# Scores of a 64-key cross-attention on 64-row tiles of TensorE instead of the full 128-row array

## The reference

```python
q = hidden_state @ Wq + bq          # 32 query heads of 32
k = encoder_hidden_state @ Wk + bk  # 8 key heads of 32
scores = jnp.einsum('bkgld,bksd->bkgls', q, k) * scale
scores = scores + encoder_attention_mask[:, :, None, :, :]
attn = jax.nn.softmax(scores, axis=-1)
```

## Time and profile before

| | us |
|---|---|
| median of 3 runs | 1916.51 |
| lowest, highest | 1906.94, 1917.58 |
| the profiled execution's own time | 1914.38 |
| its span in the trace | 1912.6 |
| mean granted TensorE clock of the span | 0.978 |

### The profile page before, as it was taken

One profiled execution on the slowest core, in us unless ns is written; L12 is line 12 of the kernel. 1 busy time (PEld: TensorE's weight loads), 2 busy tenths in 40 slices (PEclk: granted clock), 3 DMA queues, 4 the chain that ended last, 5 costly groups with the idle time before them and its releaser, 6 DMA issues.

```text
span 1912.6 us, 22864 instructions
## 1 busy us (share of the span) xinstructions
PE 1791.6 (94%) x8832; PEld 1486.5 (78%) x8832; DVE 1073.9 (56%) x1070; ACT 578.7 (30%) x664; POOL 1029.4 (54%) x576
## 2 busy tenths in 40 slices
PE   5999999999988899999999967999999999999998
PEld 5788888888876778788778856887788778877887
DVE  6888888888867344444444454345534554455432
ACT  3444444444434432333233312113211321122110
POOL 2677777777759745565654664225522552254221
PEclk9999999999999999999999988999999999999999
DMA  8423332333263466556757745414341434142110
GB/s 206 111 75 82 81 83 70 80 85 77 52 194 113 132 220 205 193 189 207 240 188 233 228 136 154 154 67 126 95 154 66 128 93 154 66 135 86 66 56 33
DMA packets 250476, 244.48 MB, mean 128 GB/s; under 512 B 61952, under 2 KB 205440, under 8 KB 250368
## 3 DMA queue, kind: packets, MB, share of 16 engines
q1 hardware_dynamic: 249216, 241.97, 41.6%
q10 hardware_dynamic: 1152, 1.05, 0.2%
HBM read 157.99 MB, written 84.93 MB: 127 GB/s over the span
## 4 chain that ended last, share of the span: by engine, by line
PE 54%; DVE 20%; issue 9%; ACT 6%; DMA 4%; POOL 3%; SPq 3%; ACTq 0%; DVEq 0%
PE ps L53 17%; PE ps L54 16%; PE ps L55 16%; DVE small L998 3%; DVE pr L1021 3%; ACT pr L765 3%; DVE pT0r L1032 2%; DVE pT1r L1032 2%; DVE xT0r L928 2%; PE ps L672 2%; ACT ot L759 2%; DVE xT1r L928 1%; PE ps L616 1%; DVE x2r L1104 1%; PE ps L624 1%
## 5 line engine op out<-in xcount | busy, mean ns | idle before, releaser
L1299 POOL TENSOR_TENSOR prob<-prob,small 128x1024 f32<-128x1024 f32 x32 | 61.1, 1908 | 397.9 <-DVE small L1115 397.9
L1235 POOL TENSOR_TENSOR pr<-pr,small 128x1024 f32<-128x1024 f32 x64 | 122.0, 1906 | 100.8 <-DVE small L1027 100.8
L1111 DVE SCALAR_TENSOR_TENSOR prob<-ps,bias 128x1024 f32<-128x1024 f32 x32 | 39.1, 1222 | 227.6 <-PE ps L55 227.6
L866 ACT CAST x2Th<-x2r 128x1024 fp32r<-128x1024 f32 x32 | 33.6, 1050 | 424.7 <-DVE x2r L1104 424.7
L1251 POOL TENSOR_TENSOR xb<-xb,bo 128x1024 f32<-128x1024 f32 x32 | 79.4, 2483 | 150.0 <-DMA xb<-in_x_dram 149.7
L1230 POOL TENSOR_TENSOR pr<-pr,small 128x1024 f32<-128x1024 f32 x64 | 124.0, 1937 | 34.4 <-DVE small L1002 34.2
L998 DVE TENSOR_REDUCE small<-pr 128x16 f32<-128x1024 f32 x64 | 78.1, 1220 | 90.7 <-ACT pr L765 90.7
L1074 DVE TENSOR_TENSOR y<-ps,xb 128x512 f32<-128x512 f32 x64 | 43.9, 687 | 126.1 <-PE ps L55 122.9
L53 PE MATMUL ps<-wo0h,oc0l 128*128 128x512 f32 x256 | 104.2, 407 | 1.7 <-DVE wo0l L952 1.7
L1043 DVE TENSOR_TENSOR y<-y,gam 128x1024 f32<-128x1024 f32 x32 | 51.6, 1612 | 92.2 <-ACT y L798 92.2
L53 PE MATMUL ps<-wo0h,oc1l 128*128 128x512 f32 x256 | 103.1, 403 | 0.0
(11 more groups left out here) (318 smaller groups left out, 5526.1 us busy)
## 6 DMA issues: line engine op xcount, KB each, us to landing
o_scratch<-ot SPq DMA_DIRECT2D x256, 64.0 KB, 1.8
ocr<-o_scratch SPq DMA_DIRECT2D x16, 1024.0 KB, 7.0
xb<-in_x_dram SPq DMA_DIRECT2D x32, 512.0 KB, 6.5
x_scratch<-y SPq DMA_DIRECT2D x32, 512.0 KB, 4.7
a_scratch<-ost SPq DMA_DIRECT2D x64, 256.0 KB, 3.3
b_scratch<-ost SPq DMA_DIRECT2D x64, 256.0 KB, 4.6
xd<-x_scratch SPq DMA_DIRECT2D x128, 128.0 KB, 2.9
raw<-b_scratch SPq DMA_DIRECT2D x64, 256.0 KB, 7.5
```

Source lines behind the costliest of these rows:

```text
L1235: nc.gpsimd.tensor_tensor(heads(v), heads(v), mx.unsqueeze(2).to_broadcast([P, TPB * GRP, KEYS]), ALU.subtract)\
L1299: nc.gpsimd.tensor_tensor(prob[:], prob[:], mx1.unsqueeze(2).to_broadcast([P, H1, KEYS]), ALU.subtract)\
```

## The change

The 128-row matmul of a token tile is split in two by rows: rows 0 to 63 hold heads 0 and 1, rows 64 to 127 hold heads 2 and 3. Each half is a matmul of 64 rows and 128 moving columns (two heads of 64 keys), issued alternately, three terms each, in the same order of terms. A unit has 24 such matmuls. The half r writes bank r of `S`, so the order in a unit's two banks becomes (head j, tile m, key), which is the order of `pr`; DVE's addition of the mask reads and writes in that order, with the mask of the block repeated over heads.

```diff
--- before.py
+++ after.py
@@ -542,8 +542,13 @@
                     pe.wait_ge(k_ld[v % 2], 16 * GRP * (v // 2 + 1))
                     after(pe, s_read, v - 1)
                     for m in range(TPB):
-                        last = three(nc, S[v % 2][:, 256 * m:256 * (m + 1)], [qs[v % 2][x][:, m] for x in (0, 1)],
-                                     [kb[v % 2][:, :, x] for x in (0, 1)], True, True)
+                        for i, (x, z) in enumerate(((1, 0), (0, 1), (0, 0))):
+                            for r in range(2):
+                                rows = slice(2 * HD0 * r, 2 * HD0 * (r + 1))
+                                last = nc.tensor.matmul(S[v % 2][:, HALF * r:HALF * (r + 1)]
+                                                        .rearrange("p (j m s) -> p m j s", j=2, m=TPB)[:, m],
+                                                        qs[v % 2][x][rows, m], kb[v % 2][rows, 2 * r:2 * r + 2, z],
+                                                        start=i == 0, stop=i == 2)
                     last.then_inc(scores, 1)
                 if u < UNITS:
                     query(range(4, KT))
@@ -1018,10 +1023,10 @@
                     if v % KT == 0:
                         dve.wait_ge(mask_ld, 16 * (t + 1))
                     dve.wait_ge(scores, v + 1)
-                    nc.vector.tensor_tensor(p[:].rearrange("p j m s -> p m j s"),
-                                            S[v % 2].rearrange("p (m j s) -> p m j s", m=TPB, j=GRP),
-                                            mask[t % 2][:].unsqueeze(2).to_broadcast([P, TPB, GRP, KEYS]), ALU.add)\
-                        .then_inc(s_read, 1)
+                    nc.vector.tensor_tensor(p[:].rearrange("p j m s -> p j (m s)"),
+                                            S[v % 2].rearrange("p (j c) -> p j c", j=GRP),
+                                            mask[t % 2][:].rearrange("p m s -> p (m s)").unsqueeze(1)
+                                            .to_broadcast([P, GRP, TPB * KEYS]), ALU.add).then_inc(s_read, 1)
                     dve.wait_ge(s_read, v + 1)
                     after(dve, centered, v)
                     nc.vector.tensor_reduce(mx, p[:].rearrange("p j m s -> p (j m) s"), AX_X, ALU.max).then_inc(maxed, 1)

```

## The result

| | us |
|---|---|
| changed kernel, median of 20 runs (lowest to highest) | 1914.72 (1908.74 to 1921.52) |
| kernel before, median of 20 runs | 1910.37 (1905.81 to 1917.58) |
| ratio, 95% interval | 1.0025 (1.0013 to 1.0036) |
| span of the profiled execution, mean granted clock | 1911.4, 0.974 |

The change makes the kernel slower by 2.5 to 6.9 us, 4.35 between the medians, against 1.6 forecast. The time lies in the range, and the sign is the forecast's.

The account below looks back on a forecast made before the run. DVE, ACT and POOL, at 17.13 us a pair of slots, were taken to bound the kernel, hiding PE's growth to 17.04. Six PE-bound slots add 1.6: 1914.4 becomes 1916.0, with 2.1 for the median 1918; range 1909 to 1928.

Parts of the forecast that it names:

- What bounds the kernel: First layer's slots: DVE, ACT and POOL set 17.13 us a pair of slots; PE needs 16.52 and has 0.61 spare.
- the ring: Cycle of DVE, ACT and POOL work in a pair of slots, mask addition to token transpose, repeating every 17.13 us.
- The block: A unit's scores on PE: 12 pairs of 64-row matmuls at 0.108 us, 1.30 in place of 1.44, a gain of 0.14.
- In and out: Entering and leaving the 64-row tiles on PE loses 0.20 us each way, 0.40 in each of 64 units.
- The cover: PE's wait for the queries' low part hides its longer slot over 23 pairs; without it 0.26 a slot, 12 us.
- The mask addition: DVE's addition in the new order, 64 times: 0 to +2.9 us, taken as 0.
- The size: Whole kernel: 1.6 us slower, from 0.26 in each of some six slots that PE bounds.
- the pair at 0.118: First rival, score block: PE just becomes the bound, pair of slots 17.28, +5.8 us, 1922; chance 0.20.
- the full gain at 0.066: Second rival, score block: matmul pairs take 0.066 us, only six slots gain, -1.5 us, 1915; chance 0.08.
- the pair that costs two steps: Third rival, score block: a matmul pair takes 0.216 us, pair of slots 19.62, about +70 us, 1988; chance 0.11.
- the clock: Fourth rival: PE's idler array lets its clock fall in each third pair of slots, +16 us, 1934; chance 0.04.

Follow-up runs that it names:

- one term: Kernel before with only the high by high product of the scores, 4 matmuls of 256 columns a unit in place of 12: 1905.65 us.
- the swap: Kernel before with ACT's exponential ahead of the output copy in each slot, nothing changed on PE: 1889.63 us.
- two blocks: Changed kernel with a unit's scores in two blocks of 12 matmuls, six full-row projection matmuls between them: 1926.36 us.
- full-row cut: Kernel before with each full-row score matmul of 256 columns cut into two of 128 columns, 24 a unit, no tiles: 1971.68 us.
- the loops exchanged: Changed kernel with, per token tile, the three terms of rows 0 to 63 written before the three of rows 64 to 127: 1914.52 us, one execution.
- the old order of the mask addition: Changed kernel with DVE's mask addition walking in the order token tile, head, key, tiles unchanged: 1918.54 us, one execution.
- one term with the swap: Kernel before with only the high by high score product and ACT's exponential ahead of the output copy: 1882.03 us.
- the swap with tiles: Changed kernel with ACT's exponential ahead of the output copy: 1907.68 us.

## Why the prediction was right

- *What bounds the kernel*: right, and shown from three sides. Less work on PE leaves the period at 17.12 (one term), a shorter ring without a change on PE takes it to 16.52 (the swap), and a longer PE raises it only once its slot passes the ring (two blocks, 17.68).
- *The block*: 12 pairs at 0.108 were expected and 0.112 measured. The full-row cut shows the same 0.112 without any tiling. That the load sets it fits the 0.11 of an exposed load, and is argued, not shown by a run.
- *In and out*: 0.20 us each way was read from the tables, and an unwaited block shows the same way in: the full matmul that starts at 524.22 ends 0.227 later, and the first pair, loaded from 524.54 on, begins 0.11 after that, a gap of 0.20. The way out was taken from the tables at 0.20 and is 0.14 here. The experiment with two blocks puts the real addition at 0.31 a block. That the sum came out so close, 8.53 against 8.52, is in part luck: the underestimate of the pairs (12 x 0.004 = 0.05) and the overestimate of the way out (0.06) have opposite signs.
- *The cover*: right. The 23 pairs of slots lost 17.17 - 17.13 = 0.04 us each, while PE still had 0.11 us to spare in each. Without the cover the tiles cost 18 us.
- *The mask addition*: nothing, as taken; 1.173 against 1.176 us over the same stretch.
- *The size*: too small. 1.6 us forecast, 4.35 measured (2.5 to 6.9). In the profiled executions the last scores start 606.86 - 602.61 = 4.25 us later. Of it, 1.1 us are the ring's 0.04 (the token transposes, a term that the sum did not have), 0.95 us lie between 513.19 and 546.34, where PE bounds, as forecast, and 1.8 us are there by slot 8, at 121.02 against 119.25. Half of this last part, 0.96 us, is there before the first scores (47.93 against 46.97), and 0.82 of it already at the first query projection, where nothing was changed (below). The rest, 0.5 us, is at the end of the layer.
- *Rivals*: the pair at 0.118, the full gain at 0.066, the pair that costs two steps, and the clock are all out: 0.112, 0.112, 0.112, and a mean clock of 0.974 against 0.978. The first rival was nonetheless near. Its condition, a pair of slots over the ring's, fails by 17.13 - 17.06 = 0.07 us.

The first matmul of the query projection before:

```profile
38.68 0.40 PE L53 MATMUL ps<-xT0h,wq0l 128*128 128x512 f32 x1
```

and after:

```profile
39.50 0.47 PE L53 MATMUL ps<-xT0h,wq0l 128*128 128x512 f32 x1
```

Most of this 0.82 us is not an accident of one execution. The profiled executions of the six kernels with 24 score matmuls a unit (the changed one, full rows, and the other four with tiles) start this matmul at 39.17 to 39.50 us, those of the four with 12 or 4 at 38.68 to 38.80. The prediction had no term for this, and its cause stays open.

## What to carry to other kernels

A busy share of 94% on an engine does not say that a shorter operation on it pays: look for the period in the starts of a repeated instruction and compare it with the stretch in which nothing is waited for. The steady slots here held 0.61 us of wait in 17.13, enough to hide a step that became 0.27 us a slot worse, and DVE's long wait for the exponential pointed to the swap of two ACT operations that was worth 1%. At 128 columns a pair of 64-row tiles brought a step of 0.120 us down to 0.112 and no further, about what an exposed weight load takes (0.11), and the ways in and out came on top, some 0.3 us a block.

## What the runs showed of the hardware

An fp32r matmul of 128 columns with its own weights takes 0.112 us at the full clock, about as long as an exposed load of 128 columns delays its matmul (498.86 to 498.97, 0.11). The Trainium skill, "TensorE: Matmul & The Clock Gate", LDWEIGHTS (loading the stationary operand), gives columns / 1.2, which for 128 is an estimate of 107 ns, and at the full clock the 0.11 agrees. At the lower level of the clock (granted 0.50 over 66.0 to 68.9 us in the changed kernel) the pairs come further apart:

```profile
66.32 0.66 PE L548 MATMUL ps<-kb,qs0h 64*128 64x128 f32 x4
...
68.24 0.66 PE L548 MATMUL ps<-kb,qs0h 64*128 64x128 f32 x4
...
66.04 0.32 PEld L548 LDWEIGHTS ps<-kb,qs0l 64*128 64x128 f32 x2 [4.15 <-DVE qs0l L1041]
66.21 0.58 PEld L548 LDWEIGHTS ps<-kb,qs0h 64*128 64x128 f32 x4
```

Nine pairs take 1.92 us, 0.213 each, and the exposed load ahead of them delays its matmul by 66.21 - 66.04 = 0.17. Both grow as the clock falls, which that formula does not say. But the pace is now longer than the exposed load's delay, so that the load alone sets the pace is not shown at this level.

The same page, The mechanism (of row and column tiling), says that matmuls start and end strictly in program order. With the loops exchanged the trace shows otherwise across row tiles: the low product of rows 64 to 127 starts beside that of rows 0 to 63, ahead of two matmuls that stand before it in the program. Here 12 steps remain 12, where I had expected 16 from a strict order.

What stays open is why DVE's token transpose takes 2.08 us in the kernel before and 2.13 in the changed one. It reads and writes neither the scores nor PSUM; it is at 2.13 also with the old order of the mask addition, and in the kernel with the swap and no tiles. Three more kernels have 2.07 to 2.10 (two blocks and one term with the swap 2.07, the swap with tiles 2.10), so neither the tiles nor the swap alone decides it. The cause was not separated.
